# A fused layer kernel: in the attention stage, the statistics of the second normalisation move into the step of the projection, and all that follows them moves one step forward

## The reference, cut to what matters

```python
x = x + mamba(layernorm(x))                    # 16 sequences x 1024 tokens x 256
n = layernorm(x)
ln1 = ln(n, w1, b1);  qkv = ln1 @ qkv_weight.T
# attention over groups of 16 rows (the first axis), causal, 16 heads of 16, 8 key/value heads
hid = n + softmax(mask(q @ k.T / 4)) @ v @ proj_weight.T
m = ln(hid, w2, b2)                            # the second normalisation
probs = softmax(m @ router_weight)             # 8 experts, the best 2 are kept
x = x + hid + moe(m, probs)                    # each token goes through its two experts
```

## Time and profile before

| what | value |
|---|---|
| median of 3 runs (lowest, highest) | 6447.79 us (6447.11, 6450.78) |
| profiled execution, its own time | 6448.49 us |
| its span | 6446.7 us |
| mean granted TensorE clock | 0.978 |
| busy share: PE, PEld, DVE, ACT, POOL | 94%, 61%, 66%, 55%, 78% |

### The profile page before, as it was taken

The page is one execution under the profiler, slowest core; times in us unless marked ns, Lnnn a source line. Parts: engine busy times, 40 slices in busy tenths (PEclk is TensorE's granted clock), DMA queues, the critical chain, the costliest instruction groups (busy, mean ns, idle before and its releaser), DMA issues. The chain is left out here.

```text
span 6446.7 us, 78759 instructions
## 1 busy us (share of the span) xinstructions
PE 6085.9 (94%) x25311; PEld 3902.1 (61%) x25312; DVE 4238.7 (66%) x5700; ACT 3553.7 (55%) x6456; POOL 5053.7 (78%) x3844
## 2 busy tenths in 40 slices
PE   7999999999999999999998699996999999999999
PEld 3444444444444444444443488885888888888887
DVE  6999999999999999999999567787000000000000
ACT  5677676767676776777676478873222222222221
POOL 6999999999999999999999687762445555554554
PEclk9999999999999999999999999998999999999999
DMA  3545554555555555555544334443666666666554
GB/s 122 165 164 170 165 171 162 164 168 168 165 164 172 165 166 166 170 162 165 170 166 161 99 100 124 124 128 72 180 183 181 189 185 180 189 186 179 178 169 123
DMA packets 562603, 1028.78 MB, mean 160 GB/s; under 512 B 90578, under 2 KB 256980, under 8 KB 527632
## 3 DMA queue, kind: packets, MB, share of 16 engines
q1 hardware_dynamic: 455088, 668.00, 32.6%
q0 software_dynamic: 107104, 355.74, 18.7%
HBM read 925.79 MB, written 88.08 MB: 157 GB/s over the span
## 5 line engine op out<-in xcount | busy, mean ns | idle before, releaser
L365 POOL TENSOR_TENSOR m_dbu<-m_du,m_bb 128x1024 f32<-128x1024 f32 x1024 | 2398.7, 2381 | 0.0
L743 PE MATMUL m_y_bank<-m_prod,m_ident 128*128 128x512 f32 x4096 | 1976.8, 612 | 147.3 <-POOL m_prod L374 147.3
L516 ACT ACTIVATE m_decay<-m_delta,m_a_neg 128x512 f32<-128x512 f32 x2048 | 1419.4, 695 | 725.7 <-DVE m_h L626 723.8
L743 PEld LDWEIGHTS m_y_bank<-m_prod,m_ident 128*128 128x128 f32 x4096 | 788.8, 196 | 1126.7 <-issue 907.5
L1795 DVE TENSOR_SCALAR e_ye<-e_ybank,e_share 128x256 f32<-128x256 f32 x270 | 118.2, 479 | 1768.3 <-PE e_ybank L1828 1768.3
L626 DVE TENSOR_TENSOR_SCAN m_h<-m_decay,m_h_end,m_dbu 128x512 f32<-128x512 f32 x1024 | 1258.5, 1265 | 3.6 <-ACT m_decay L516 2.5
L626 DVE TENSOR_TENSOR_SCAN m_h<-m_decay,m_dbu 128x512 f32<-128x512 f32 x1024 | 1196.2, 1204 | 12.6 <-ACT m_decay L516 12.0
L1776 ACT ACTIVATE e_a<-e_ubank 128x512 f32<-128x512 f32 x540 | 322.5, 597 | 1473.4 <-PE e_ubank L1819 1472.2
L374 POOL TENSOR_TENSOR m_prod<-m_h,m_cb 128x1024 f32<-128x1024 f32 x416 | 989.6, 2379 | 18.1 <-issue 13.7
L1819 PE MATMUL e_ubank<-e_xT,s_w 128*128 128x256 f32 x4320 | 978.4, 380 | 1.3 <-ACT e_xT L1767 1.3
L1828 PE MATMUL e_ybank<-s_w,e_a 128*128 128x256 f32 x4320 | 954.5, 379 | 0.7 <-ACT e_a L1776 0.7
(11 more groups left out here) (213 smaller groups left out, 6506.5 us busy)
## 6 DMA issues: line engine op xcount, KB each, us to landing
m_bb<-rows_bc SPq DMA_DIRECT2D x1024, 256.0 KB, 3.6
m_cv<-rows_bc SPq DMA_DIRECT2D x608, 256.0 KB, 3.8
m_cb<-rows_bc SPq DMA_DIRECT2D x416, 256.0 KB, 3.3
m_xin<-in_x SPq DMA_DIRECT2D x32, 512.0 KB, 5.6
m_xres<-in_x SPq DMA_DIRECT2D x32, 512.0 KB, 5.4
x<-m_xres SPq DMA_DIRECT2D x32, 512.0 KB, 6.0
a_xa<-x SPq DMA_DIRECT2D x64, 256.0 KB, 2.8
a_xr<-x SPq DMA_DIRECT2D x64, 256.0 KB, 3.2
```

What stands on the lines that cost most here:

```text
L365: nc.gpsimd.tensor_tensor(dbu[:, slot], du[:, q[1], p * PC:(p + 1) * PC], bb[:, slot].unsqueeze(1).to_broadcast([P, PC, T]), ALU.mult).the ...
L516: nc.scalar.activation(decay[:, cc], delta[:, r, c], ACT.Exp, scale=a_neg[:, c, n:n + 1]).then_inc(decay_done, 1)
L743: ins = nc.tensor.matmul(y_bank[:, cc], ident[:], prod[:, slot, cc], start=False, stop=(n == NS - 1))
```

## The change

The lags of the statistics, the normalisation and the router each fall by one, and VectorE's order within a step changes: `normalise_2` and `statistics_2` now stand behind `take_proj` and ahead of `scale_output`. There are 89 steps instead of 90.

```diff
-    RESIDUAL, PROJ, STATS2, NORM2, ROUTER = 21, 22, 23, 24, 26
+    RESIDUAL, PROJ, STATS2, NORM2, ROUTER = 21, 22, 22, 23, 25
     STEPS = ITEMS + ROUTER
...
             for step in range(STEPS):
                 for k in items(step, PROBS):
                     inverse(k)
-                for k in items(step, NORM2):
-                    normalise_2(k)
                 for k in items(step, SCORES):
                     centre(k)
                 for k in items(step, PROJ):
                     take_proj(k)
+                for k in items(step, NORM2):
+                    normalise_2(k)
+                for k in items(step, STATS2):
+                    statistics_2(k)
                 for k in items(step, OUTPUTS):
                     scale_output(k)
                 for k in items(step, STATS):
                     statistics(k)
                 for k in items(step, VTURN):
                     turn_values(k)
-                for k in items(step, STATS2):
-                    statistics_2(k)
```

## The result

| | before | after |
|---|---|---|
| median of the runs beside each other (lowest, highest) | 6450.32 us (6447.11, 6453.02) | 6472.6 us (6470.08, 6476.83) |
| profiled execution, its own time; span | 6448.49; 6446.7 us | 6476.83; 6475.1 us |
| mean granted TensorE clock | 0.978 | 0.974 |

What follows compares the result with a forecast made beforehand. TensorE's instruction sum was taken to bound the middle steps, a round of VectorE and GpSimd the last ones. 0 + 2.7 + 9.9 - 2.6 = +10.0, plus 6 for the clock: +16, 6464 us, range 6453 to 6475.

Steps and rivals of the forecast that it cites:

- term A: Middle steps, to step 65: one norm2 transpose group and one route move into full TensorE steps, +1.3 us.
- term B: Steps 66 to 73: a vanished store wait gives back the middle steps' cost; together 0, bounds -2 and +3 us.
- the round of 7.67: Steps 66 to 73: closed chain normalise_2, transposes, projection, take_proj, 7.67 us, shorter than VectorE's own period of 7.89.
- term C: Steps 74 to 77: the closed round makes four steps 24.5 us instead of 21.84, +2.7 us.
- term D: Steps 78 to 85: closed round of 5.47 us against 4.23, eight times 1.24, +9.9 us.
- term E: The last item: 8.7 us from last take_proj to last logits copy instead of 11.34, -2.6 us.
- term F: End of attention stage: TensorE's granted clock falls for two and a half steps at +2.4 us each, +6 us.
- rival 2: End of attention stage: clock falls early and stays low, nine steps at +2.4 us, 6480 us; chance 8%.
- my own case: Last steps: a closed round of 5.47 us and a clock that falls part of the time, +11 to +22; 55%.
- 1 (clock holds, 6458): Last steps: the clock does not fall, so only the +10.0 us without clock change, 6458 us; chance 20%.
- 3 (cost in the middle): Middle steps: the new order costs each of 40 steps, at 0.5 us +20 on top, 6484 us; chance 5%.
- 4 (the round does not close, 6440): Last steps: no closed round, GpSimd waits go, not slower: -7.5 us, 6440 us; chance 12%.

Runs made afterwards that it cites:

- experiment 1: Changed kernel with normalise_2 put back ahead of centre and take_proj, the shorter lags kept: 6443.75 us, ratio 0.9988 to the kernel before.
- experiment 7: Changed kernel with TensorE's norm2 transposes, their copy and the router one step later: 6441.48 us, 0.9986; again on another chip 6439.13 us, 0.9982.
- experiment 6: Changed kernel with normalise_2 between the two halves of take_proj: 6459.94 us, ratio 1.0015 to the kernel before.
- experiment 2: Changed kernel with statistics_2 back at the end of VectorE's step: 6475.52 us, ratio 1.0037 to the kernel before.
- experiment 4: Changed kernel with three discarded matmul calls behind each projection from step 77: 6458.76 us, ratio 1.0012 to the kernel before.
- experiment 8: As experiment 1, with four discarded matmul calls in step 86 before the last transposes: 6442.53 us, ratio 0.9988 to the kernel before.
- experiment 9: As experiment 7, with four discarded matmul calls in its last step before the last transposes: 6440.43 us, ratio 0.9984 to the kernel before.

## Why the prediction was right in sign and short in size

**The middle steps, term A (+1.3).** From step 22 to step 65 before 462.82 us (3787.57 to 4250.39), after 464.19 (3788.88 to 4253.07): +1.37. The new order costs nothing more there, as forecast: the middle step is 10.8 us in both, and in the step at 4101 the new normalise_2 ends at 4103.1, 3.0 us ahead of the transposes that need it.

**Steps 66 to 73, term B.** I had it give back A and no more. From step 65 to 73 (4253.07 to 4318.04, before 4250.39 to 4318.32) it is 64.97 instead of 67.93 us: -2.96. The wait for the store is gone and nothing took its place: from 4272 to 4318 VectorE has no wait at all, and its step is 7.78 us on average, so it and not the round of 7.67 sets the pace, though by 0.1 us only. A + B is -1.6 and lay inside its bounds of -2 to +3.

**Steps 74 to 77, term C (+2.7).** 4318.04 to 4342.51 is 24.47 us, forecast 24.5; against 21.84 before: +2.63.

**Steps 78 to 85, term D (+9.9).** At the full clock a turn is 5.51 us (5.52 in steps 76 to 77, 5.51 with the three calls of filling), forecast 5.47: 8 x (5.51 - 4.23) = +10.2. Experiments 1 and 7, which open the round in two different ways, have 4.01 and 3.56 us, and experiment 6, which shortens it by one instruction of 0.6, has 4.92. This shows that it is the round, and not, say, traffic on GpSimd.

**The last item, term E (-2.6).** 9.17 us from 4403.98 to 4413.15 instead of 11.34: -2.2. I took 8.7 of 7.8 to 9.2, and it came out at the upper bound, because all of it ran at the low clock: from the last normalise_2 to the last copy 5.16 us (4407.99 to 4413.15), as before.

**The clock, term F (+6): the step that was mis-sized.** Its price per step was nearly right: a low turn is 8.2 to 8.3 us, +2.8, where I had +2.4. The number of steps was wrong. I took two and a half, arguing that the low stretch in the mamba stage had ended as soon as TensorE was dense again. That was a misreading to begin with: in that row TensorE is busy for all 3.40 us at 0.50. And in the closed round it is never dense again: the low clock lengthens the projection, but VectorE's part of the round, 2.08 us of idle, comes again in every step. So F in the profiled execution is 61.47 - 8 x 5.51 = +17.4 us, 6.2 full low steps' worth, near rival 2 (the clock falls early and does not return, +22, to which I gave 8%). In the median it is less: 22.3 less the other terms, -1.6 + 2.6 + 10.2 - 2.2 = 9.0, leaves 13.3, and the filling that keeps the clock gave 13.8 back (16.8 against experiment 2). With F at 13.5 the sum would have been 6471 us on the base that I used. The other terms sum to 9.0 where I had 10.0, partly because their misses cancel (-1.6 in A + B against +0.3 and +0.4 in D and E). And +22.3 is the far end of what I called my own case (+11 to +22): the mechanism was mine, the share of low steps was rather that of rival 2.

The rule quoted with that term, from the Trainium skill, "TensorE: Matmul & The Clock Gate", section "HAM oscillation — how this bites in real kernels", gave F = 0, since each gap is shorter than the one it names. The traces do not agree: gaps of 2.08 us, repeated in every step, kept the mean clock at 0.62, and gaps of 1.2 to 1.65 us (one call of filling) at 0.77 to 0.89. Gaps of 0.8 us, before and with three calls, left it at 1.00. Of the two kinds of rows that I had to weigh, the one with 1.93 us pointed the right way. But the length of one gap does not settle it: in experiment 6 a projection behind 1.49 us of idle ran at the full clock and the next one, behind 1.49 too, did not. What decides between them is open.

**The rivals.** 1 (clock holds, 6458): what experiment 4 made true by force, 6458.76, or +7.7 against the kernel before on its chip where the rival had +10.0. 3 (cost in the middle): no. 4 (the round does not close, 6440): not in this kernel, but it is what experiments 1 and 7 build, and its sum of -7.5 was good: -7.3 and -8.6.

**Why the intended gain did not show.** One step less is worth 2.2 us at the end, and the vanished store wait 3.0. Both are there. Eight turns of a closed round at +1.28 and the clock at +13 to +17 outweigh them. The gain is had if the transposes don't wait for a normalisation that waits for the same step's projection. Both ways of doing that are faster than the kernel before by 0.1 to 0.2% (the intervals of experiments 1, 7, 8 and 9 all lie below 1); which of them is the best, the runs do not tell. Not tried: the old lags with only normalise_2 moved behind take_proj; with two buffers of `hid`, take_proj would wait for a normalise_2 that stands behind it.

## What to carry to other kernels

When a pipeline's lag is shortened, look at its emptying end, where the engines have nothing else to do: list the instructions from one engine's product round to its next one, with the waits in both directions. If the chain closes within one step, its sum is the step. What opens it again is a single piece that stands ahead of the wait for the other engine's product, or one step later. If TensorE is the one that idles in such a round, price the round a second time at the low clock and count all its steps, not a few.

## What the runs showed of the hardware that I had not expected

- TensorE's clock falls in a loop of short idles that come again in each step: after an idle of 1.64 us at 4344.49 the next projection already ran partly at the low clock (3.15 us instead of 2.13), and from the take_proj before it the granted clock was 0.62 on average for 61 us. The same idle of 1.49 us was followed by the full clock in one step of experiment 6 and by the low one in the next.
- Idle rests of TensorE can be worth filling with discarded work: six recorded matmuls (1.46 us) in each of nine steps took 13.8 us off the changed kernel (16.8 against experiment 2 on the same chip).
- One f32 matmul call of 256 columns stands in the trace as two records of 0.23 to 0.27 us each; a reckoning from the number of calls gives half of what it costs.
